# Writing out the loops of the first and the recurrent stage of a four-layer graph network kernel

## What is computed

```python
x = _layernorm(x + _L0_gnn_ref(x, adj, W, bias, prelu_a))      # prelu(adj @ (x @ W) + bias)
x = _layernorm(x + _L1_gnn_ref(x, adj, weight, bias))          # adj @ (x @ W) + bias
x = _layernorm(x + _L2_gnn_ref(x, adj, nodemask, ...))         # five steps of a GRU, below
x = _layernorm(x + _L3_gnn_ref(x, adj, W1, b1, W2, b2, ...))   # five node groups, two graph convolutions each
# L2, with A = (adj != 0):
for l in range(5):
    m = h @ weight[l]
    agg = einsum('bij,bid->bjd', A, m)
    h = gru_cell(agg, h, w_ih, w_hh, b_ih, b_hh)
```

## Time and profile before

| | us |
|---|---|
| median of 3 runs | 1122.16 (1120.86 to 1122.92) |
| the profiled execution | 1123.02 |
| its span, first to last instruction | 1121.0 |
| PE busy | 996.7 |
| DVE busy | 887.8 |
| POOL busy | 805.1 |
| ACT busy | 796.7 |

### The profile page before, as it was taken

How to read it: one execution, slowest core, us unless ns; L and a number is a source line. 1 busy time by engine, 2 the same in 40 slices (tenths; PEclk the granted TensorE clock), 3 DMA queues, 4 the chain that set the end, 5 groups by cost and what they waited for, 6 DMA issues and landing times.

```text
span 1121.0 us, 21146 instructions
## 1 busy us (share of the span) xinstructions
PE 996.7 (89%) x6010; PEld 600.6 (54%) x6010; DVE 887.8 (79%) x2447; ACT 796.7 (71%) x1375; POOL 805.1 (72%) x879
## 2 busy tenths in 40 slices
PE   3699999395999999999998999999999999877884
PEld 2599998242345544444554554454455454466763
DVE  4599999464677888889898897887889977767895
ACT  1378888373678787887887878777788876736554
POOL 0589999374458888786796887887779777678353
PEclk9699999598999999999999999999999999988897
DMA  7133332224454444335425424433443543312323
GB/s 166 42 111 113 111 101 65 57 48 79 53 91 89 70 94 85 76 70 101 85 56 103 86 56 95 84 70 81 84 83 63 107 66 71 74 31 60 83 76 83
DMA packets 294971, 90.25 MB, mean 81 GB/s; under 512 B 222291, under 2 KB 294764, under 8 KB 294892
## 3 DMA queue, kind: packets, MB, share of 16 engines
q1 hardware_dynamic: 281066, 88.55, 36.9%
q10 hardware_dynamic: 13826, 0.85, 0.9%
HBM read 28.58 MB, written 8.81 MB: 33 GB/s over the span
## 4 chain that ended last, share of the span: by engine, by line
PE 53%; DVE 19%; issue 10%; POOL 8%; ACT 4%; DMA 2%; ACTq 2%; DVEq 0%; SPq 0%; POOLq 0%
PE psum L1277 14%; PE psum L1272 13%; PE psum L1273 13%; PE psum L1301 5%; DVE st L890 4%; POOL zh L637 3%; PE psum L1352 3%; DVE x L901 2%; DVE mv L894 2%; ACTq L758 2%; DVE ws L1037 2%; PE psum L1367 2%; DMA hnp<-htp 2%; DVE ot L1184 1%; DVE ws L1027 1%
## 5 line engine op out<-in xcount | busy, mean ns | idle before, releaser
L637 POOL TENSOR_TENSOR zh<-zw,ht 128x512 f32<-128x512 f32 x160 | 203.3, 1271 | 41.7 <-ACT zw L824 38.2
L596 POOL TENSOR_TENSOR htp<-ht,htp 128x512 f16<-128x512 f32 x128 | 148.1, 1157 | 87.6 <-ACT htp L785 87.4
L1272 PE MATMUL psum<-htp,wh_hi 128*128 128x512 f16 x480 | 184.0, 383 | 25.5 <-DMA htp<-hxp 14.7
L1272 PE MATMUL psum<-pth,wx_hi 128*128 128x512 f16 x480 | 184.9, 385 | 14.0 <-ACT pth L767 14.0
L1277 PE MATMUL psum<-ptl,wx_hi 128*128 128x512 f16 x480 | 184.1, 384 | 5.2 <-DVE ptl L1109 4.3
L1273 PE MATMUL psum<-pth,wx_lo 128*128 128x512 f16 x480 | 184.4, 384 | 0.0
L1277 PE MATMUL psum<-htp,wh_hi 128*128 128x512 f16 x480 | 183.9, 383 | 0.0
L1273 PE MATMUL psum<-htp,wh_lo 128*128 128x512 f16 x480 | 183.8, 383 | 0.0
L1083 DVE SCALAR_TENSOR_TENSOR rt<-psum,bhn,rt 128x512 f32<-128x512 f32 x160 | 119.8, 748 | 65.8 <-ACT rt L797 65.7
L824 ACT ACTIVATE zw<-psum,brz,unscale 128x512 f32<-128x512 f32 x160 | 124.1, 776 | 53.6 <-PE psum L1277 53.5
L1109 DVE SCALAR_TENSOR_TENSOR ptl<-psum,pth 128x512 f16<-128x512 f32 x160 | 110.2, 689 | 61.6 <-ACT pth L767 61.5
(11 more groups left out here) (170 smaller groups left out, 1955.0 us busy)
## 6 DMA issues: line engine op xcount, KB each, us to landing
adj<-in_adj_dram SPq DMA_DIRECT2D x32, 256.0 KB, 2.9
x<-in_x_dram SPq DMA_DIRECT2D x32, 256.0 KB, 3.3
adjr<-in_adj_dram SPq DMA_DIRECT2D x32, 256.0 KB, 3.1
out_dram<-yo SPq DMA_DIRECT2D x8, 768.0 KB
hnp<-htp SPq DMA_TRANSPOSE x128, 3.1
out_dram<-xq SPq DMA_DIRECT2D x32, 50.0 KB
v<-in_L_gnn_W_dram SPq DMA_DIRECT2D x2, 640.0 KB, 5.4
x3q<-x SPq DMA_DIRECT2D x16, 50.0 KB
```

Of the source, the lines that this page charges most:

```text
L596: nc.gpsimd.tensor_tensor(HT_LO[s % 2], HT[s][:, :], HT_HI[s % 2], ALU.subtract).then_inc(b_htl, 1)
L637: nc.gpsimd.tensor_tensor(ZH[s % 2][:, :], ZW[s % 2][:, :], HT[s][:, :], ALU.mult).then_inc(b_zh, 1)
L1272: mm(dst, w_h[:, col:col + P], h[:, :], start=start, stop=False)
```

## The change

The loops go. `run_a` and `run_b` no longer take an engine, every step and every round is written out in Python, and SP's loop over `load_a` is written out as well. Addresses and wait values that came from registers are constants. The order of the work on every engine stays as it was.

```diff
-        def run_a(eng, role):
+        def run_a(role):
             peeled, total = steps_a(role)
             for k in range(8):
                 peeled(k)
-            with eng.Fori(2, STEPS_A // 4) as j:
-                for m in range(4):
-                    role(j * 4 + m, m, lambda lag: True)
+            for k in range(8, STEPS_A):
+                role(k, k % 4, lambda lag: True)
             for k in range(STEPS_A, total):
                 peeled(k)
...
-        def run_b(eng, slot, unrolled=False):
+        def run_b(slot):
 
             def body(it, slots):
                 for j in slots:
                     slot(lambda lag: item(j - lag, it))
             body(0, range(-EARLY, TURN))
-            body(1, range(TURN))
-            if unrolled:
-                for it in range(2, ROUNDS - 1):
-                    body(it, range(TURN))
-            else:
-                with eng.Fori(2, ROUNDS - 1) as it:
-                    body(it, range(TURN))
+            for it in range(1, ROUNDS - 1):
+                body(it, range(TURN))
             body(ROUNDS - 1, range(TURN + 4))
...
-            with sp.Fori(1, STEPS_A // 4) as j:
-                for m in range(4):
-                    load_a(j * 4 + m, m, lambda lag: True)
+            for k in range(4, STEPS_A):
+                load_a(k, k % 4, lambda lag: True)
```

More of the change, by code:

```diff
@@ L511, in slot_b @@
                     sp.dma_start_transpose(blocks(FNP[s]), FTP[p][:, :]).then_inc(b_tf[p], 16)
-            run_b(sp, slot_b, unrolled=True)
+            run_b(slot_b)
             for k in range(STEPS_C + 2):
@@ L581, in step_a @@
                       .then_inc(a_nm1, 1)
-            run_a(pool, step_a)
+            run_a(step_a)
             pool.wait_ge(a_x2, STEPS_A)
@@ L648, in slot_b @@
                     nc.gpsimd.tensor_tensor(NMB[s][:, :], NMB[s][:, :], minus[:, 0:G4], ALU.mult).then_inc(b_nm, 1)
-            run_b(pool, slot_b)
+            run_b(slot_b)
             def step_c(k, has):
@@ L731, in step_a @@
                     last.then_inc(a_x2, 1)
-            run_a(act, step_a)
+            run_a(step_a)
             n2v = n2[:, :].rearrange("p (q c) -> p q c", c=2 * SLOTS)
@@ L831, in _ @@
             act.wait_ge(a_x2, STEPS_A)
-            run_b(act, slot_b)
+            run_b(slot_b)
             def apply_c(k, some):
@@ L1044, in step_a @@
                     norm(WS1[p], ST1, MV1[p], G4, a_w1, k - 2, a_bs1, a_mv1)
-            run_a(dve, step_a)
+            run_a(step_a)
             def slot_b(at):
@@ L1118, in slot_b @@
                           .then_inc(b_sxl, 1)
-            run_b(dve, slot_b)
+            run_b(slot_b)
             def step_c(k, has):
@@ L1256, in step_a @@
                     four(bank[4], lambda i: cols(YT1, i), lambda i: w1_sb[:, :], a_z1, bias_kn[1])
-            run_a(pe, step_a)
+            run_a(step_a)
             W2 = 2 * SLOTS
@@ L1326, in _ @@
             pe.wait_ge(a_x2, STEPS_A)
-            run_b(pe, slot_b)
+            run_b(slot_b)
             def step_c(k, has):
```

## The result

The changed kernel takes 1107.09 us (median of 4 runs, 1105.66 to 1108.55) against 1122.2 before (1120.86 to 1122.92): 15.1 us less, ratio 0.9867 with a 95% interval of 0.985 to 0.9884. The forecast was 1109.0, in a range of 1105.5 to 1114.

A forecast was written before the change was run, and what follows sets the result against it. PE, busy 89% of the span, sets stage B's pace, with DVE's gaps at back edges making it wait. 13.48 - 0.80 + 2.0 - 1.5 = 13.2 us gained gives 1109.0 us, range 1105.5 to 1114.

The forecast's parts named there:

- The back edges of stage B, 13.48 us: Stage B, rounds 2 to 5: each loses what it has over round 6's 88.49 us, 13.48 us gained in all.
- So the gap comes with the branch: DVE's line 1062 at stage B's borders: idle where a branch goes back, none between rounds 6 and 7; not `adjr`'s load.
- fetched once and kept, the others' is fetched again and again as it is: Stage B's loop code: PE's queue moves none in round 3, the other engines' queue q14 moves five packets.
- What the others have lies beside it, and goes too.: Stage B: branches of PE, ACT and POOL lie beside DVE's gap, which PE waits for; they go too.
- Round 2's own 0.80: Round 2's first sixteen slots, 71.62 us against round 3's 70.82: lost while PE's code is fetched, forecast to stay, -0.80 us.
- Packets of PE's code, 15 at 0.10: Rounds 3 to 6: 15 new code packets share the transposes' DMA engines, 0.10 us each, 1.5 us lost.
- The rival by the price of a branch: Stage B's gap has another cause; only the branches' own execution goes, estimated 1 us for nine: 1121 to 1122 us, chance 0.03.
- the chain's 3.55 us: DVE's sequencer at line 318, the loop's line, at 590.03: nothing follows for 3.55 us, then line 318 again.
- Stage A, 2.0 us: Stage A's five back edges, bounded by 1.6 and 2.17 us; nothing hides them before stage B, so 2.0 us gained.
- Not all steps take 4.76 as I had said: Stage A, where DVE sets the pace: the sign that its steps would all take 4.76 us once written out.
- The range: Range for 8 in 10, 1105.5 to 1114 us; own bounds 1105.8 (15.5 us gain, with spread) and 1112.7 (10.2 us).

The follow-up runs named there:

- a_straight: Changed kernel with stage B's loops kept on all four engines, only stage A written out: 1104.6 us, ratio 0.9833 to the kernel before.
- head216: Kernel before, all loops kept, head of DVE's loop over rounds 2 to 6 put at place 216 of a 256-instruction block: 1104.74 us, ratio 0.9846.
- dve_straight: Changed kernel with loops put back on PE, ACT and POOL in both stages, DVE written out: 1105.87 us, ratio 0.9858 to the kernel before.
- after_2: The changed kernel run once more, unaltered, on the same chip as two other versions: 1107.07 us, ratio 0.9869 to the kernel before.
- head232: Kernel before, all loops kept, head of DVE's loop over rounds 2 to 6 put at place 232 of a 256-instruction block: 1119.77 us, ratio 0.9993.
- place 0: Kernel before, all loops kept, head of DVE's loop over rounds 2 to 6 put at the start of a 256-instruction block: 1112.89 us, ratio 0.9924.

## Why the prediction was right, and what in it was not

**The back edges of stage B, 13.48 us.** The size was right: rounds 2 to 6 lost 12.49 us, where 13.48 - 0.80 - 1.5 = 11.2 was forecast. Where the time goes was right too, DVE's wait before line 1062. The cause was right by half: "So the gap comes with the branch". It takes a branch back, and it takes a place of DVE's loop at which the branch's target is no longer held. The same branches, on the same engine, cost a round nothing in `a_straight` and `head216`. The number came out because a program without the branch has no gap wherever its code lies; that DVE's loop lay badly in the kernel before was luck for the forecast, and in a kernel where it lies well the same change would have gained nothing in stage B. The comparison that I rested on, borders with a branch back against borders without one, separates the two only if each back edge costs alike wherever the code lies. And the row that told otherwise was there: I read PE's body as "fetched once and kept, the others' is fetched again and again as it is", and took the five q14 packets of round 3 for the way loops are. Moving DVE's loop alone takes 15 of the 16 packets of rounds 3 to 5 away, so ACT's and POOL's bodies (226 and 169 instructions of the built program, too short to touch more than three pieces of 128) were kept all along.

**"What the others have lies beside it, and goes too."** Shown by `dve_straight`: with the three other engines' back edges left in, rounds take 88.5 us.

**Round 2's own 0.80.** Forecast to stay. In the changed kernel round 2 takes 88.61, as the others, so it did not. It was left in the kernels with loops that keep the old code up to there: 88.80 with `head216`, 88.96 with `dve_straight`. Over all kernels without a gap in it, round 2 takes 88.60 to 89.38, each time with four or five packets of PE's code, so the 0.80 was no fixed price of that round. That it hangs on where packets fall against the transposes is argued, not shown.

**Packets of PE's code, 15 at 0.10.** 12.5 instead of 11.2 came since this and the 0.80, 2.3 us together, were too high for this trace. Rounds 2 to 6 hold 443.44 - 5 x 88.49 = 1.0 us over the clean pace in it, for 22 packets: 0.05 each. In the trace of `after_2` it is 444.27 and 1.8: 0.08 each, so the forecast was near. The worst case in the first is one round, the sixth, in which PE waits 0.43 for `hnp` (timeline of PE):

```profile
846.16 0.62 PE L1294 MATMUL psum<-a,hnp 128*128 128x128 f16 x8 [0.43 <-DMA hnp<-htp]
```

The rule of the Trainium skill (Runtime: NRT & Kernel Launch, Instruction fetch mechanics) that crossing a block of code is mostly hidden would have made this zero. The two traces lie between the rule and my 0.10: 0.05 and 0.08. The same section warns that a taken branch whose target isn't in the two pages held forces a fetch before the engine goes on. That is what `head216` and `head232` show, with 13.2 us over rounds 2 to 6 between a target that is held and one that isn't; the size of what is held is another here, four pieces of 128 instructions on DVE. The question it asks (is the target still held?) is the one the prediction left out.

**The rival by the price of a branch.** About 108 ns for a compare-and-branch (the Trainium skill, Advanced Engine Details and Errata, Control Flow Timing) was weighed against the chain's 3.55 us and dismissed. Both cases exist. With `head216` DVE's sequencer takes 0.3 us from its branch to the next instruction, more than the page's 108 ns, and none of it can be seen in a round (88.50, against 88.49 for round 6 in the earlier trace rows). In the kernel before the same step takes 3.4 to 3.6 us. The rival's price was that of a branch whose target is held, and here it wasn't.

**Stage A, 2.0 us.** The stretch up to stage B shrank by 2.47. From line 1020 to line 1020 over the 24 steps it is 80.72 to 195.67, so 114.95 against 116.41: 1.46 us less. The steps begin 0.96 us later than before, and 1.97 us are gained between them and stage B, which the forecast did not have. Not all steps take 4.76 as I had said:

```profile
176.28 0.72 DVE L1020 SCALAR_TENSOR_TENSOR ws<-un,nalpha,ws 128x512 f32<-128x512 f32 x1
...
181.15 0.31 DVE L887 BATCH_NORM_AGGREGATE mv<-st 128x2 f32<-128x6 f32 x3 [0.22 <-issue]
181.38 0.72 DVE L1020 SCALAR_TENSOR_TENSOR ws<-un,nalpha,ws 128x512 f32<-128x512 f32 x1
```

Two steps take 5.04 and 5.10. The same two have it in every kernel in which DVE's stage A is written out, so it goes with the code. In `dve_straight` packets of q14 leave at 93.8 and 181.0 us, within a microsecond of the two delays, but also at 115.3, 137.1 and 159.2 us, where no step is longer; so the border of a piece alone isn't the cause, which stays open. Over the eight traces with DVE's stage A written out the first slot of stage B is at 221.6 us on the mean, over the six with the loop at 223.8: 2.2 us.

**What the forecast did not have.** Round 7 took 0.92 less. `after_2`, the same kernel, has 89.44 us there against the 87.39 of the first trace, more than before's 88.31, so this is no gain of the change. The difference lies in two slots behind a point where SP spends 6.6 to 6.9 us on issuing stage C's first eight loads ahead of a transpose: PE then waits 3.0 us for `hnp` in the first trace, 3.8 in `after_2` and 2.4 before, and ACT idles 1.01 and 1.34 us for "issue" in the latter two; the cause of that was not tried.

**The range.** Its lower end is set off a slip: 15.5 us off 1120.86 are 1105.4, not 1105.8. The measured 1107.09 is inside by either.

## What to carry to other kernels

Before a loop is written out because its back edge shows a gap, look which engine has it and whether that engine's code packets go on in the steady rounds. Here one packet in three rounds meant that all bodies were held and the branches free, and five a round that one wasn't (code that is written out moves packets too, 13 in three rounds of the changed kernel). If the body is one that can be held, its place is the cheaper cure: 216 instead of 232 gave all that writing out two stages gave. And code that lies ahead of a loop is part of its cost: an edit in one stage moved another stage by 13 us without touching it, so a comparison of two versions should look at that first.

## What the runs showed that was not expected

A loop of 287 instructions costs 13 us over four back edges or nothing, by sixteen places of its head. An end at 503 is good and one at 519 is bad; that alone would fit two blocks of 256, but the packets show pieces of 128 instructions, of which DVE keeps four with the one ahead. A jump forwards to code that isn't held costs the same once: 3.24 us of DVE and 4.5 us of the round with place 0, against 0.15 us of DVE with 216. And PE's body, with the more than 1,000 matmuls and weight loads of a round, was never fetched again in rounds 3 to 5 of any kernel that looped it, where DVE's of 287 was.
